# Two small transposes per pair of graphs moved from TensorE to VectorE, and a rounding copy from VectorE to ScalarE

## The reference

```python
qk = X @ Wqk; q, k = split(qk); v = X @ Wv            # layer 0
agg = einsum('bij,bjd->bid', adj, k * mask)
w = 1/16 * mask * einsum('bid,bid->bi', q, agg)        # one weight per node
x = layernorm(x + softmax(w, axis=1)[:, :, None] * v)

query, keyt, value = x @ Wq.T + bq, x @ Wk.T + bk, x @ Wv.T + bv   # layer 1
weight = adj * exp(query @ keyt.T); weight /= sum(weight, axis=2)
x = layernorm(x + weight @ value)
```

## Time and profile before

| what | value |
|---|---|
| median of 3 runs (lowest, highest) | 296.91 us (296.63, 296.96) |
| the profiled execution's time | 296.95 us |
| its span in the trace | 295.2 us |
| busy share of the span: PE, PEld, DVE, ACT, POOL | 97%, 90%, 80%, 76%, 75% |
| mean granted TensorE clock | 0.994 |

### The profile page before, as it was taken

One profiled execution on the slowest core, in us unless ns is written; L12 is line 12 of the kernel. 1 busy time (PEld: TensorE's weight loads), 2 busy tenths in 40 slices (PEclk: granted clock), 3 DMA queues, 4 the chain that ended last, 5 costly groups with the idle time before them and its releaser, 6 DMA issues.

```text
span 295.2 us, 7074 instructions
## 1 busy us (share of the span) xinstructions
PE 287.0 (97%) x2012; PEld 266.6 (90%) x2012; DVE 235.1 (80%) x728; ACT 224.7 (76%) x539; POOL 220.3 (75%) x269
## 2 busy tenths in 40 slices
PE   7999999999999999999999999999999999999991
PEld 7789999999999999999999999999999999999980
DVE  1478888888878888888888888788887888888784
ACT  3455768788788878878887887878788787887763
POOL 1556988877888877788887778978777897877331
PEclk9999999999999999999999999999999999999997
DMA  6921234322344432324443232444323243210102
GB/s 231 338 91 37 89 92 126 93 95 85 109 124 125 125 96 86 95 96 125 125 125 92 86 101 94 125 125 125 93 85 92 103 125 125 89 55 25 50 36 107
DMA packets 19165, 31.26 MB, mean 106 GB/s; under 512 B 2128, under 2 KB 6608, under 8 KB 19152
## 3 DMA queue, kind: packets, MB, share of 16 engines
q1 hardware_dynamic: 19152, 31.11, 34.2%
HBM read 22.71 MB, written 8.39 MB: 105 GB/s over the span
## 4 chain that ended last, share of the span: by engine, by line
PE 94%; DMA 2%; issue 1%; DVE 1%; ACT 0%; POOL 0%; SPq 0%; POOLq 0%; DVEq 0%
PE ps L866 25%; PE ps L868 24%; PE ps L867 24%; PE ps L967 9%; PE ps L949 5%; DMA p<-params 2%; PE ps L917 1%; PE ps L923 1%; PE ps L889 1%; PE ps L1101 1%; PE ps L972 1%; DVE x L649 0%; PE ps L928 0%; PE ps L936 0%; POOLq L36 0%
## 5 line engine op out<-in xcount | busy, mean ns | idle before, releaser
L866 PE MATMUL ps<-w_hi,xt_hi 128*128 128x512 f32 x124 | 49.9, 402 | 0.0
L868 PE MATMUL ps<-w_hi,xt_lo 128*128 128x512 f32 x124 | 48.8, 393 | 0.0
L867 PE MATMUL ps<-w_lo,xt_hi 128*128 128x512 f32 x124 | 48.5, 391 | 0.0
L452 ACT ACTIVATE x<-x_sum,shift,rstd 128x256 f32<-128x256 f32 x60 | 32.9, 595 | 17.0 <-POOL shift L377 17.0
L363 POOL TENSOR_TENSOR edge_lo<-edge,edge_hi 128x256 fp32r<-128x256 f32 x29 | 21.5, 740 | 29.5 <-ACT edge_hi L532 29.5
L296 POOL TENSOR_TENSOR x1b<-x,bv_all 128x512 f32<-128x512 f32 x31 | 40.2, 1297 | 2.6 <-DVE x L805 1.7
L350 POOL TENSOR_TENSOR xt_lo<-xt_raw,xt_hi 128x512 fp32r<-128x512 f32 x31 | 40.1, 1294 | 1.8 <-ACT xt_hi L434 1.8
L467 ACT ACTIVATE z<-ps,z_bias 128x256 f32<-128x256 f32 x62 | 26.0, 472 | 19.7 <-PE ps L868 19.7
L374 POOL TENSOR_TENSOR rstd<-var_eps,minus_half 128x4 f32<-128x4 f32 x31 | 33.2, 1071 | 9.3 <-DVE var_eps L783 9.3
L866 PE MATMUL ps<-wv_hi,x1t_hi 128*128 128x258 f32 x124 | 37.8, 305 | 0.0
L357 POOL TENSOR_TENSOR x_lo<-x_raw,x_hi 128x512 fp32r<-128x512 f32 x28 | 36.2, 1293 | 0.0
(11 more groups left out here) (162 smaller groups left out, 880.3 us busy)
## 6 DMA issues: line engine op xcount, KB each, us to landing
xt_raw<-xt_pairs SPq DMA_DIRECT2D x32, 256.0 KB, 2.7
x_raw<-x_pairs SPq DMA_DIRECT2D x32, 256.0 KB, 2.7
out_pairs<-x SPq DMA_DIRECT2D x31, 256.0 KB, 2.0
adjt<-adjt_pairs SPq DMA_DIRECT2D x32, 129.0 KB, 2.1
p<-params SPq DMA_DIRECT2D x1, 770.0 KB, 6.7
p<-params SPq DMA_DIRECT2D x1, 512.0 KB, 3.8
p<-params SPq DMA_DIRECT2D x1, 256.0 KB, 4.7
out_pairs<-x SPq DMA_DIRECT2D x2, 128.0 KB, 1.8
```

The costliest lines, as they stand in the source:

```text
L452: last = nc.scalar.activation(out[:, graph(g)], in_[:, graph(g)], ACT.Identity, bias=shift[r % 2][:, layer, g:g + 1], scale=rstd[r % 2][:, ...
L866: nc.tensor.matmul(out, s_hi, m_hi, start=first, stop=False)
L867: nc.tensor.matmul(out, s_hi, m_lo, start=False, stop=False)
L868: return nc.tensor.matmul(out, s_lo, m_hi, start=False, stop=last)
```

## The change

`w_col` goes: the accumulators are read into the first two columns of PSUM bank 7 (`w_col_ps`), and `transpose_w` becomes four VectorE transposes of 32 x 32 blocks, from the four groups of 32 partitions into four column blocks of one PSUM row tile (`w_row_ps`). `p_row` is written to PSUM (`p_row_ps`), and four VectorE transposes of 32 x 32 blocks bring it into `p_col`, now 32 columns wide, directly. The copy `p_col` out of PSUM goes. PE's `transpose_w` and `transpose_p` go. PE's `aggregate` of the next pair, and the transpose of `x1` at the end, now wait for `w_row_done`. `x1t_hi` is made by ScalarE out of PSUM, right behind `x1t`, in all slots but slot 0. The tile used for the warm-up matmuls is renamed.

```diff
-        w_col = sb("w_col", [128, 2])
-        p_row = sb("p_row", [128, 128])
-        p_col = sb("p_col", [128, 2])
+        warm = sb("warm", [128, 128])
+        p_col = sb("p_col", [128, BLOCK])
...
+        w_col_ps = agg_ps[:, 0, 0:BLOCK]
+
         def w_row_ps(r):
-            return yv_ps(r)[0:2, 0, 0:NODES]
+            return yv_ps(r)[0:BLOCK, 1, 0:NODES]
...
-        def p_full_ps(r):
-            return yv_ps(r)[:, 1, 0:NODES]
-
-        def p_col_ps(r):
-            return p_full_ps(r)[:, 0:2]
+        def p_row_ps(r):
+            return yv_ps(r)[0:BLOCK, 1, NODES:2 * NODES]
...
                     act.wait_ge(x1t_done, t + 1)
                     nc.scalar.copy(x1t[:, :, :, :], x1t_ps).then_inc(x1t_copied, 1)
+                    if r != 0:
+                        act.wait_ge(val_done, t)
+                        nc.scalar.copy(x1t_hi[:, :, :, :], x1t_ps).then_inc(x1t_hi_done, 1)
...
-                                               w_col[:, g:g + 1]).then_inc(w_done[g], 1)
+                                               w_col_ps[:, g:g + 1]).then_inc(w_done[g], 1)
+
+            def transpose_w(u, r):
+                for g in range(2):
+                    dve.wait_ge(w_done[g], u + 1)
+                for b in range(0, NODES, BLOCK):
+                    block = nc.vector.transpose(w_row_ps(r)[:, b:b + BLOCK], w_col_ps[b:b + BLOCK, :])
+                block.then_inc(w_row_done, 1)
...
             def sum_x1(u, r):
                 dve.wait_ge(p_col_done, u + 1)
-                nc.vector.tensor_copy(p_col[:, :], p_col_ps(r)).then_inc(p_copied, 1)
...
                 if exists(t + 2):
                     for g in range(2):
                         weight(t + 2, r + 2, g)
+                    transpose_w(t + 2, r + 2)
...
-                    nc.vector.tensor_scalar(p_row[0:2, :], exp_row_ps(r + 2), inv_sum[:, 0:1], None, ALU.mult)\
+                    nc.vector.tensor_scalar(p_row_ps(r + 2)[0:2, :], exp_row_ps(r + 2), inv_sum[:, 0:1], None, ALU.mult)\
                         .then_inc(p_row_done, 1)
+                    dve.wait_ge(p_row_done, t + 3)
+                    for b in range(0, NODES, BLOCK):
+                        block = nc.vector.transpose(p_col[b:b + BLOCK, :], p_row_ps(r + 2)[:, b:b + BLOCK])
+                    block.then_inc(p_col_done, 1)
...
                 if exists(u - 1):
                     pe.wait_ge(agg_copied, u)
+                    pe.wait_ge(w_row_done, u)
...
-                if exists(t + 2) and r > 0:
-                    transpose_w(t + 2, r + 2)
                 if r == DRAIN:
                     pe.wait_ge(x1_done, t + 2)
-                    pe.wait_ge(agg_copied, PAIRS)
+                    pe.wait_ge(w_row_done, PAIRS)
...
                 if r != DRAIN:
-                    transpose_p(t + 2, r + 2)
                     transpose_next(t, r)
```

More of the change, by code:

```diff
@@ L26 @@
 SPLIT = 4
+BLOCK = 32
 def exists(pair):
@@ L142, in build @@
         ident_zeroed, ident_ready, consts_ready = sem("ident_zeroed"), sem("ident_ready"), sem("consts_ready")
-        p_row_zeroed = sem("p_row_zeroed")
+        warm_zeroed = sem("warm_zeroed")
         bqk_done, bqk_summed, ones_ready = sem("bqk_done"), sem("bqk_summed"), sem("ones_ready")
@@ L163, in build @@
         x1_sum_done, w_done = sems("x1_sum_done", 2), sems("w_done", 2)
-        row_max_done, inv_sum_done, p_row_done, p_copied = sem("row_max_done"), sem("inv_sum_done"), sem("p_row_done"), sem("p_copied")
+        row_max_done, inv_sum_done, p_row_done = sem("row_max_done"), sem("inv_sum_done"), sem("p_row_done")
         stats1_done, x1t_hi_done, x1t_lo_done = sem("stats1_done"), sem("x1t_hi_done"), sem("x1t_lo_done")
@@ L403, in slot @@
                     add_value_bias(r + 1)
-            nc.gpsimd.memset(p_row[:, :], 0.0).then_inc(p_row_zeroed, 1)
+            nc.gpsimd.memset(warm[:, :], 0.0).then_inc(warm_zeroed, 1)
             nc.gpsimd.memset(ident[:, :], 0.0).then_inc(ident_zeroed, 1)
@@ L568, in slot @@
                     act.wait_ge(row_max_done, t + 3)
-                    nc.scalar.activation(exp_row_ps(r + 2), w_row_ps(r + 2), ACT.Exp, bias=neg_max[:, 0:1],
+                    nc.scalar.activation(exp_row_ps(r + 2), w_row_ps(r + 2)[0:2, :], ACT.Exp, bias=neg_max[:, 0:1],
                                          accum_out=exp_sum[:, 0:1]).then_inc(row_exp_done, 1)
@@ L612, in both_stats, with split_x1t @@
                                           source[:, :].rearrange("p (g d) -> p d g", g=2))
[L614 to L618, removed]
+            def split_x1t(t, r):
+                if r == 0:
+                    dve.wait_ge(x1t_copied, 1)
+                    nc.vector.tensor_copy(x1t_hi[:, :, :, :], x1t[:, :, :, :]).then_inc(x1t_hi_done, 1)
                 dve.wait_ge(x1t_hi_done, t + 1)
@@ L624, in sum_x1 @@
                 dve.wait_ge(p_col_done, u + 1)
-                nc.vector.tensor_copy(p_col[:, :], p_col_ps(r)).then_inc(p_copied, 1)
                 if exists(u - 2):
                     dve.wait_ge(x1_done, u - 1)
-                dve.wait_ge(p_copied, u + 1)
                 for g in range(2):
@@ L752, in slot @@
                 if r == 0:
-                    split_x1t(t)
+                    split_x1t(t, r)
                 if exists(t + 1):
@@ L815, in slot @@
                     dve.wait_ge(w_row_done, t + 3)
-                    nc.vector.tensor_reduce(neg_max[:, :], w_row_ps(r + 2), AX.X, ALU.max, negate=True).then_inc(row_max_done, 1)
+                    nc.vector.tensor_reduce(neg_max[:, :], w_row_ps(r + 2)[0:2, :], AX.X, ALU.max, negate=True).then_inc(row_max_done, 1)
                 if r == 0:
@@ L908, in project @@
                     mm = project_half(u, r, g, k)
-                    if r == 2 and g == 0 and k == 0:
-                        transpose_p(1, 1)
                 mm.then_inc(yv_done[g], 1)
[L913 to L923, removed]
             def fold_scores(m):
@@ L1067, in slot @@
                     values(x1t_hi, x1t_lo, 0)
-                    if r == 0:
-                        transpose_w(2, 2)
                     values(x1t_hi, x1t_lo, 1).then_inc(val_done, 1)
-                    if r == DRAIN:
-                        transpose_p(t + 2, r + 2)
                     pe.wait_ge(z_copied, t + 1)
@@ L1081, in slot @@
                 if r != DRAIN:
-                    transpose_p(t + 2, r + 2)
                     transpose_next(t, r)
-            pe.wait_ge(p_row_zeroed, 1)
+            pe.wait_ge(warm_zeroed, 1)
             for _ in range(WARM_UP):
-                nc.tensor.matmul(ps[:, 0, 0:128], p_row[:, :], p_row[:, :], start=True, stop=True)
+                nc.tensor.matmul(ps[:, 0, 0:128], warm[:, :], warm[:, :], start=True, stop=True)
             pe.wait_ge(wqk_loaded, 16)
@@ L1112, in _ @@
             fold_scores(0)
-            transpose_w(0, 0)
             fold_scores(1).then_inc(at_done, 1)
             aggregate(1, 1)
-            transpose_p(0, 0)
             project(1, 1, 0)
@@ L1119, in _ @@
             fold_biases()
-            transpose_w(1, 1)
             aggregate(2, 2)
```

4 lines of the change are left out of this document (removed).

## The result

The changed kernel takes 312.38 us, median of 4 runs (311.65 to 312.61), against 296.92 for 4 runs of the kernel before (296.63 to 296.96): ratio 1.052, 95% interval 1.0507 to 1.0532. Forecast were 292.9 and a range up to 298.0: wrong in sign, and outside the range. The rival that fits is "DVE becomes the pace", at more than the price that I gave it.

A forecast was written before the change was run, and what follows sets the result against it. The prediction took PE (TensorE) as the bound, with DVE next. Its terms, -6.3 in the slots, +1.6 at the start and +0.6 at the end, sum to -4.1 us: 296.95 becomes 292.9, range 290.3 to 298.0.

The forecast's parts named there:

- DVE becomes the pace: Rival, chance 0.21: the two groups of four transposes on DVE make the kernel slower, 300.2 us at 0.25 us per transpose.
- What bounds the kernel now: Whole run: PE sets the pace, 94% of the last-ending chain, 8.62 us a slot; DVE is next in line.
- What PE loses: PE's weight and softmax transposes: 0.225 us a slot saved, slot 8.40, 6.3 us over 28 slots.
- What DVE gains (T): Eight 32x32 transposes per pair on DVE: T, the price of each start to start, taken as 0.21 us, without overlap.
- Does DVE still fit?: One DVE round in the new order: 6.62 + 8T, or 8.30 us, under PE's 8.40.
- Does the loop through PE fit?: From the queries' end through softmax and x_sum to the projection: 3.44 us against PE's 3.47, fits by 0.03.
- ScalarE's new copy: x1t_hi between x1t and edge_hi on ScalarE: some 0.5 us, covered by waits, costed at nothing.
- The two ends: Start and end of the run: DVE's transposes lengthen the chains there, 1.6 us at the start and 0.6 at the end.

The follow-up runs named there:

- same_quadrant: The changed kernel with all four transposes of a group reading and writing partitions 0 to 31, other partitions' values left out; 294.25 us, ratio 0.9908.
- late_variance_lo_ps: The changed kernel with x1t_lo read from PSUM and neg_mean and var_eps moved behind x1t_lo; 309.01 us, ratio 1.0405.
- lo_ps: The changed kernel with x1t_lo reading its input from PSUM instead of SBUF; 312.91 us, ratio 1.0518.
- w_only: The changed kernel with the softmax row turned by PE again; weight transposes stay on VectorE, the x1t_hi copy on ScalarE; 299.15 us, ratio 1.0076.

## Why the prediction was wrong, step by step

**What bounds the kernel now**: right. PE was the pace, DVE next.

**What PE loses**: right in kind, a little too large. In same_quadrant, where both transposes are gone and PE runs without waits, most slots are 8.41 to 8.53, the mean 8.494: 0.13 less than before and not 0.225. Some 0.06 of the rest went into the turn of `x1`, whose four matmuls took 0.415 until the next start instead of 0.358; why is not shown.

**What DVE gains (T)**: the step was right that nothing overlaps, and mis-sized. T is 0.238 for the weights and 0.221 for the softmax rows, 1.87 for all eight with their gaps against 8 x 0.21 = 1.68: 0.19 a slot. That alone would not have turned the sign, and T was not the whole margin, as the text said: with T = 0.21 the loop found in late_variance_lo_ps would take 8.90 - 0.19 = 8.71 (an estimate from its rows), more than the 8.62 of before. The text also gives two times for T = 0.19, 292.9 and 292.0; its sum supports the lower.

**Does DVE still fit?** This step failed. The sum had DVE at 8.30 and it took 9.01; the slot is 0.60 over the forecast 8.40, and 28 x 0.60 = 16.8 are most of the 19.5 us between forecast and measurement. The missing 0.71 are: 0.19 from T; 0.12 around the accumulators, whose read into PSUM lasts 134 ns instead of 84 and is followed by 0.10 of gap instead of 0.03; 0.37 in `neg_mean`, a row that I took over at its old length of 0.16; 0.03 of small differences. The term of `neg_mean` came from copying durations out of the old order into a new one, in which the neighbour on GpSimd had moved.

**Does the loop through PE fit?** It counted one loop, from the end of the queries to the projection, and was too short there by 0.15 - 0.04 = 0.11. It left out the second loop: `x_sum`, projection, second weight, both groups of transposes, `x_sum`. That one takes 8.90 and would have held the slot there even with `neg_mean` at its old length.

**ScalarE's new copy**: costed at nothing. Right alone (297.00 against 296.95). In the whole change it saves DVE 0.45 a slot and brings `neg_mean` into `edge_lo` once the softmax rows are on DVE; the net is a gain of (1.0637 - 1.0520) x 297 = 3.5 us. The cost that I looked for, PE waiting for `edge_lo`, did not come; the waits for GpSimd that did come are for `adjm_lo` and do not set the time, as lo_ps shows.

**The two ends**: right in kind, half the size. Rows of PE's timeline in the kernel after:

```profile
20.20 1.10 PE L897 MATMUL ps<-x_raw,adjm 128*128 128x256 f32 x4 [1.97 <-DVE ps L613]
21.14 0.92 PE L943 MATMUL ps<-ident,x 128*128 128x128 f32 x4
...
22.29 0.63 PE L874 MATMUL ps<-w_lo,xt_hi 128*128 128x512 f32 x1
22.72 0.63 PE L875 MATMUL ps<-w_hi,xt_lo 128*128 128x512 f32 x1
...
292.42 0.39 PE L873 MATMUL ps<-x1t_hi_a,at_hi 128*128 128x256 f32 x1 [0.73 <-DVE x1t_lo_a L682]
```

The first four are at the start, +3.1 instead of +1.6. PE's aggregation of pair 2 waits 1.97 for the transposes of the weights and starts 2.0 later than before (18.21 there). The rest is a term that the prediction does not have, TensorE's clock. Behind that wait, from 21.3 to 24.7, the granted clock is 0.50, the lower of its two levels (1.2 GHz), and the projection's matmuls start 0.43 apart instead of 0.23. From the turn of `x1` at 21.14 to the end of the projection PE takes 4.80, where it took 3.32 before at a clock of 1.00: 1.5 more, of which the work that has left PE gives 0.4 back by the next turn. All five profiled kernels with both groups at full length have such a stretch at the start; w_only, whose wait there is 1.15, and the others have none. That the longer wait brought the clock down is read from this and was not tested by itself. The last row is at the end, +1.7 instead of +0.6: `x1t_lo_a`, which feeds PE, stands behind the last group of transposes on DVE. I had costed the transposes only for the chain through `x_sum`, not for what else was queued behind them.

**Rival "DVE becomes the pace"**, at 0.21: it named the right engine, and not the reason. It used T alone as its lever. With the measured 1.87 for all eight its own sum gives a round of 8.49 and about 296.1 us, still a little faster; even its 300.2 at T = 0.25 is 12 us short. That DVE became the pace came from the other terms above.

## What to carry to other kernels

The transposes on VectorE that walked over the four groups of 32 partitions ran strictly one behind another (starts 0.22 to 0.24 apart, against 0.11 within one group). Cost such a row of small instructions at full length plus a gap, and check each loop that their queue closes, not only the sum of the engine. An engine that is 20% idle before a change may have none of it to give: its waits were where other engines' data came late, and a duration copied from the old order holds only if what runs beside it on the other engines stays put (`neg_mean`: 0.16, then 0.52). Moving half of the work, reading `x1t_lo` out of PSUM and shortening the loop that the work lengthens brought 1.1%, where moving all of it cost 5.2%.

## What the runs showed of the hardware

- A transpose of 32x32 f32 on VectorE took 225 ns from PSUM to PSUM and 207 ns from PSUM to SBUF when each began at another group of 32 partitions, with starts 0.24 and 0.22 apart; and 187 and 172 ns when all began at the same one, with starts 0.11 apart.
- A 128x4 `neg_mean` of 0.16 took up to 0.53 beside GpSimd's subtraction of two SBUF tiles, and ended 0.02 to 0.03 after it each time.
- GpSimd's power of 128x4 elements (`rstd`) took 1.02 us beside a VectorE subtraction with one input in PSUM, and 1.32 beside the same one with both inputs in SBUF.
- Behind a wait of TensorE of 1.97 us at the start the granted clock was 0.50 for 3.4 us, and matmuls of 512 columns stepped 0.43 instead of 0.23; behind one of 1.15 (w_only) it stayed at 1.00.
- Reading an accumulator into PSUM took 134 ns, into SBUF 84.
- From the end of VectorE's `x_sum` to the matmul that it releases were 0.15 us, and that matmul's step was 0.31 instead of 0.23.
